# An attention kernel whose sets of chunks no longer cross batches: ten sets for nine, two more chunks transposed by the matrix engine, the last moved set issued by two engines

## The chip, the cores and the metric

The kernel runs on one core of one Trainium2 chip. The metric is the device time in microseconds of one execution; the number compared is the median of several runs.

## The reference

```python
B, C, N = 4, 128, 1024          # x is (4, 128, 32, 32), seen as (B, C, N)
h = group_norm(x, 8 groups) * gn_w + gn_b
q, k, v = qw @ h + qb, kw @ h + kb, vw @ h + vb      # per batch, [C, N]
attn = softmax(q^T k / sqrt(C), axis=-1)              # [N, N] per batch
out = x + pw @ (v attn^T) + pb
```

All arithmetic is in float32. The kernel folds qw and kw into one matrix and pw into the values, so that what is left per batch is a projection g, the values v, the scores g·h, the exponentials, and the product of values and exponentials, divided by the row sums.

## The kernel before

**Chunks and steps.** The 1,024 query rows of each of the 4 batches are cut into 8 chunks of 128: 32 chunks, handled in 32 steps. Step c computes the scores of chunk c on PE (six matmuls of 512 columns into one of two PSUM buffers S), and DVE drains them (L656: adds a row term, takes the minimum, writes s_sb). ACT then takes the exponential in place (L502) and sums the row.

**Turning the exponentials.** The product with the values needs the exponentials with keys on the partitions, so each chunk must be transposed. There are two ways.
- A direct chunk is transposed by PE in 8 pieces (`transpose_probs`, L404) into two PSUM banks, which ACT (L525) and DVE (L711) copy to pair_T.
- A moved chunk is transposed by DVE within 32x32 blocks (`transpose_blocks`, L665) into blocks, and DMAs then carry the blocks to other partitions, into pT (`move_set`, L189): 16 DMAs for a set, from 4 groups a of source partitions to 4 groups j of target partitions, each of the four a with its own semaphore.

**Sets.** Consecutive chunks form sets: `SETS = (2, 4, 4, 4, 4, 4, 4, 4, 2)`. The first and the last set are direct, the seven between are moved. The sets of four begin at chunks 2, 6, 10, ..., 26, so the sets from 6, 14 and 22 cross from one batch into the next. blocks and pT each have two buffers, used by sets in turn.

**Value units.** The product of a set is computed in units of 4 matmuls with 256 columns (8 instructions each in the profile, L377 for moved sets and L350 for direct ones), one unit per chunk, 32 in all. Unit m of a moved set runs in step m + LAG, with LAG = 8, after the scores of that step; units 0 and 1 run in steps 4 and 5. In a set inside one batch the first two units read only a = 0 and 1, so they wait for the first 8 DMAs alone, and the other two read a = 2 and 3. In a set that crosses, each unit takes two chunks of one batch and all four a, so that its first unit waits for all 16 DMAs.

**After the units.** The reciprocals of the row sums (rden, one per query row) are turned by PE into rows (`turn_rden`), copied by ACT (`copy_rows`), stored to DRAM by a DMA that ACT issues (L511), and spread back over all partitions by a DMA that SP issues (`spread_rows`, L197, into rden_bc). For the last two sets PE broadcasts them instead (L340). DVE multiplies (`divide`), POOL adds the residual (`add_residual`), and SP stores the set (`store_set`, L209).

**Queues.** Each engine's instructions are in an order written out by hand, and each engine runs its own in order; semaphores join them. SP's order is, for each set, move, spread, and then the store of the set two before. DVE does in step c, in this order: any divide, the drain of c, the copy of a direct chunk, the block transpose of c - 1, then small work and at some steps the statistics of the next batch. PE does the scores of c, then value tiles or a projection where they are due, then transposes, then a unit. In steps 0, 1, 2, 6 and 7 of a batch PE has such extra work, in 3, 4 and 5 nearly none.

Of the kernel before, what the change touches and what calls it, by code (L numbers as in the profile page):

```python
# [19 lines left out]
SETS = (2, 4, 4, 4, 4, 4, 4, 4, 2)  # L20

FIRST_UNIT_STEPS = (4, 5)
LAG = 8


def build(nc, x, vectors, weights, out):
# [22 lines left out]
    with ExitStack() as ctx:  # L49
# [14 lines left out]
        def is_direct(c):  # L64
            return c < SETS[0] or c >= DIRECT

        def direct_number(c):
            return c if c < SETS[0] else c - DIRECT + SETS[0]

        def columns(n):  # L70

            return slice(P * FIRST[n], P * (FIRST[n] + SETS[n]))

        def last_batch(n):
            return (FIRST[n] + SETS[n] - 1) // CH

        def crosses(n):

            return FIRST[n] // CH != last_batch(n)

        def divided_in(c):

            for n in range(LS - 2):
                last = FIRST[n] + SETS[n] - 1
                if c == (FIRST_UNIT_STEPS[last] + 3 if n == 0 else last + LAG + 1):
                    return n
            return None
# [43 lines left out]
        pair_T = sb("pair_T", [P, KT, 2, P])  # L131
# [7 lines left out]
        sums = [ACC[:, n % 2, 0:P * SETS[n]] for n in range(LS)] + [S[:, 1, 0:PN]]  # L139
        last_sums = [ACC[:, (LS - 1) % 2, 0:UW], ACC[:, LS % 2, 0:UW]]  # L140
# [25 lines left out]
        normed_ready, last_normed, out_ready, tail_out_ready, stored = map(sem, ("normed_ready", "last_normed", "out_ready", "tail_out_ready", "stored"))  # L166
        tp_psum = sem("tp_psum")
        pair_ready = [sem(f"pair_ready{f}") for f in range(HALVES)]

        xb_flat = xb[:, :, :].rearrange("p b n -> p (b n)")  # L170
# [7 lines left out]

        block = ctx.enter_context(nc.Block())

        @block.sync
        def _(sp):
            def move_set(n):
                sp.wait_ge(blocks_ready, FIRST[n + 1] - SETS[0])
                if n > 2:
                    sp.wait_ge(part_done, FIRST[n - 1])
                for a in range(NQ):
                    for j in range(NQ):
                        sp.dma_start(moved_view(n)[Q * j:Q * (j + 1), a].rearrange("p t n -> p (t n)"),  # L189
                                     blocks_view(n)[Q * a:Q * (a + 1), j].rearrange("p t c q -> p (t c q)"))\  # L190
                          .then_inc(moved[n % 2][a], 16)
# [8 lines left out]
            def store_set(n):  # L200
                if n < SPREAD_BY_DMA:
                    sp.wait_ge(out_ready, n + 1)
                else:
                    sp.wait_ge(tail_out_ready, 2 if n == LS else 3)
                at = P * FIRST[n]
                while at < P * (FIRST[n] + SETS[n]):
                    b, first = at // N, at % N
                    width = min(N, first + P * (FIRST[n] + SETS[n]) - at) - first
                    sp.dma_start(out[b, :, first:first + width], xb[:, b, first:first + width]).then_inc(stored, 16)  # L209
                    at += width  # L210
# [20 lines left out]
            sp.wait_ge(stored, 16 * (NS + sum(crosses(n) for n in range(NS))))  # L231

        @block.tensor
        def _(pe):
            def group_deviations(b):
                pe.wait_ge(chan_ready, b + 1)
                if b > 0:
                    pe.wait_ge(gvar_ready, b)
                if b > 1:
                    pe.wait_ge(rows_ready, 2 * (b - 1))  # L240
                pe.matmul(A0[:, 0:1], deviation[:, :], chan[:, 0:1], start=True, stop=True).then_inc(dmean_psum, 1)
# [26 lines left out]
            def project_g(b, f):  # L268
# [5 lines left out]
                else:  # L274
                    pe.wait_ge(v_ready, VP * b if f == 0 else VP * b + 2)
                    pe.wait_ge(row_ready, VP * b if f == 0 else VP * b + 2)
                pe.wait_ge(h_hi_ready, HALVES * b + f + 1)
# [51 lines left out]
            def turn_rden(n):  # L329
                pe.wait_ge(rden_ready, n + 1)  # L330
                pe.wait_ge(gvar_ready, min(FIRST[n + 1] // CH + 2, B))
                if n > 0:
                    pe.wait_ge(rows_ready, n)
                pe.transpose(A0[0:SETS[n], 0:P], rden[:, n % 2, 0:SETS[n]], ident[:, :]).then_inc(rows_psum, 1)
# [9 lines left out]
            def direct_unit(n, half):  # L344
                if half == 0:
                    for f in range(HALVES):
                        pe.wait_ge(pair_ready[f], 2 if n == 0 else 4)
                    pe.wait_ge(v_ready, VP if n == 0 else VP * B)
                for t in range(PT * half, PT * (half + 1)):
                    last = pe.matmul(sums[n], v[:, FIRST[n] // CH % 3, t, :], pair_T[:, t].rearrange("p d q -> p (d q)"),  # L350
# [3 lines left out]
            def moved_unit(n, u):  # L354
                b, part, half = (FIRST[n] + u) // CH, u // 2, u % 2
                if half == 0:
                    pe.wait_ge(v_ready, VP * (b + 1))
                    if u == 0 and n > 1:
                        pe.wait_ge(normed_ready, n - 1)
                    if u == 2 and n == LS - 1:  # L360
                        pe.wait_ge(normed_ready, n)
                    for a in range(NQ) if crosses(n) else (2 * part, 2 * part + 1):
                        pe.wait_ge(moved[n % 2][a], MOVED * ((n + 1) // 2))
                probs = moved_view(n)
                if crosses(n):

                    cs = slice(2 * Q * part, 2 * Q * (part + 1))
                    to = sums[n].rearrange("p (a n) -> p a n", a=NQ)[:, :, cs]
                    probs = probs[:, :, :, cs]
                elif n == LS - 1:  # L370
                    to = last_sums[part].rearrange("p (a n) -> p a n", a=2)
                    probs = probs[:, 2 * part:2 * (part + 1)]
                else:
                    to = sums[n][:, UW * part:UW * (part + 1)].rearrange("p (a n) -> p a n", a=2)
                    probs = probs[:, 2 * part:2 * (part + 1)]
                for t in range(PT * half, PT * (half + 1)):
                    last = pe.matmul(to, v[:, b % 3, t, :], probs[:, :, t, :], start=(t == 0), stop=(t == KT - 1))  # L377
                last.then_inc(part_done, 1)

            def value_unit(m):  # L380
                n, u = set_of(m)
                if n in (0, LS):
# [4 lines left out]
            def transpose_probs(c):  # L387
                k = direct_number(c)
                pe.wait_ge(probs_ready, c + 1)
                for f in range(HALVES):  # L390
                    to = (ACC[:, f, :] if c < SETS[0] else (A1, A0)[f])
# [28 lines left out]
            for c in range(STEPS):  # L420
# [12 lines left out]
                if c - 1 in FIRST[1:LS]:  # L433
                    turn_rden(FIRST.index(c - 1) - 1)
# [4 lines left out]
                if c - 2 in range(SETS[0]):  # L439
# [5 lines left out]
                if c >= LAG + SETS[0]:  # L445
# [12 lines left out]
            value_unit(FIRST[LS - 1] + 3)  # L458

        @block.scalar  # L460
        def _(act):
# [43 lines left out]
            def copy_rows(n):  # L505
# [3 lines left out]
                act.copy(rden_rows[0:SETS[n], n % 2, :], A0[0:SETS[n], 0:P]).then_inc(rows_ready, 1)  # L509
# [3 lines left out]

            def copy_rden(n):
                act.wait_ge(bc_psum, n - SPREAD_BY_DMA + 1)
                act.wait_ge(out_ready, n - 1)
                act.copy(rden_bc[:, n % 2, 0:P * SETS[n]], S[:, 0, BANK * (n % 2):BANK * (n % 2) + P * SETS[n]]).then_inc(bc_ready, 1)

            def copy_pair(c):
# [4 lines left out]
                frm = ACC[:, 0, :] if c < SETS[0] else A1[:, :]  # L524
                act.copy(pair_T[:, 0:PT, c % 2, :], frm.rearrange("p (t q) -> p t q", t=PT)).then_inc(pair_ready[0], 1)  # L525
# [18 lines left out]
            for c in range(STEPS):  # L544
# [11 lines left out]
                if i == 4 and c - 2 in FIRST[1:LS]:  # L556
                    copy_rows(FIRST.index(c - 2) - 1)
# [4 lines left out]
                if i == 7 and c - 1 in FIRST[1:LS]:  # L562
                    copy_rows(FIRST.index(c - 1) - 1)
                if c - 2 in range(SETS[0]):
# [3 lines left out]
                exponentials(c)  # L568
            copy_pair(STEPS - 1)
# [4 lines left out]
        def _(dve):  # L574
# [71 lines left out]
            def drain_scores(c):  # L646
# [4 lines left out]
                if c > 2:  # L651
                    if is_direct(c - 3):
                        dve.wait_ge(tp_psum, HALVES * (direct_number(c - 3) + 1))
                    else:
                        dve.wait_ge(blocks_ready, c - 2 - SETS[0])
# [3 lines left out]
            def transpose_blocks(c):  # L659
                n, k = set_of(c)  # L660
                dve.wait_ge(probs_ready, c + 1)
                if n > 2 and k == 0:
                    for a in range(NQ):
                        dve.wait_ge(moved[n % 2][a], MOVED * ((n - 1) // 2))
# [9 lines left out]
            def divide(n):  # L674
                dve.wait_ge(part_done, FIRST[n] + SETS[n] if n < LS else STEPS - 2)
# [5 lines left out]
                if n in (0, LS):  # L681
# [6 lines left out]
            def add_residual(n):  # L688
                dve.wait_ge(normed_ready, LS)
                xs = xb_flat[:, columns(n)]  # L690
                dve.tensor_tensor(xs, rden_bc[:, n % 2, 0:P * SETS[n]], xs, ALU.add).then_inc(tail_out_ready, 1)

            def finish_last_moved(part):
                n = LS - 1
                dve.wait_ge(part_done, FIRST[n] + 2 if part == 0 else STEPS)
                dve.wait_ge(bc_ready, 1)
                by_rden = rden_bc[:, n % 2, 0:P * GC].rearrange("p (c a q) -> p a c q", c=GC, a=NQ)[:, 2 * part:2 * (part + 1)]
# [169 lines left out]
```

## Time and profile before

| | us |
|---|---|
| median of 3 runs | 144.14 |
| lowest and highest | 143.91 and 144.76 |
| time of the profiled execution | 144.62 |
| its span, first to last instruction | 142.6 |
| PE busy | 130.1 (91%) |
| DVE busy | 99.5 (70%) |

The trace is of one execution. Times of rows are microseconds from the start of the span. PE's granted clock is 1.00 in every stretch.

### The profile page before, as it was taken

The page shows a single profiled execution, that of the slowest core. Times are in us where ns is not written, and L with a number is a line of the kernel's source. Part 1 is how long each engine was busy: PE and PEld are TensorE (multiplying, and loading weights), DVE is VectorE, ACT ScalarE, POOL GpSimd, SP SyncE. Part 2 cuts the span into 40 slices and gives each one's busy share as a digit, 9 for nine tenths or more (in the row PEclk, how much of TensorE's full clock was granted, in tenths as well). Part 3 has the DMA queues.
Part 4 walks back from the last instruction along what each step waited for, and adds up shares of the span by engine and source line. Part 5 has one row for each costly group of instructions (what it writes and reads, how often), then busy time and mean ns, then how long its engine had stood idle before and what let it go on. Part 6 is the DMA issues. An engine that isn't in the chain of part 4 may idle for free.

```text
span 142.6 us, 2014 instructions
## 1 busy us (share of the span) xinstructions
PE 130.1 (91%) x647; PEld 109.4 (77%) x647; DVE 99.5 (70%) x172; ACT 64.9 (46%) x112; POOL 26.1 (18%) x33
## 2 busy tenths in 40 slices
PE   5999999997779999799999995999999969999990
PEld 5997878865558887688888883888888847988880
DVE  0577779989998679679697789366977893521222
ACT  4053789564566653544436845054543333512000
POOL 5043050930202061100050323000030030003000
PEclk9999999999999999999999999999999999999999
DMA  4950000005996799499824997899509987979211
GB/s 147 306 210 0 0 5 0 27 12 115 214 205 168 171 211 203 118 205 210 195 93 92 202 209 200 202 204 210 162 0 205 209 195 202 205 161 223 78 37 74
DMA packets 9565, 20.98 MB, mean 147 GB/s; under 512 B 2362, under 2 KB 4052, under 8 KB 9556
## 3 DMA queue, kind: packets, MB, share of 16 engines
q1 hardware_dynamic: 8816, 20.59, 59.3%
q10 hardware_dynamic: 740, 0.28, 0.7%
q8 instruction: 5, 0.08, 0.2%
q14 instruction: 4, 0.03, 0.1%
HBM read 4.07 MB, written 2.11 MB: 43 GB/s over the span
## 4 chain that ended last, share of the span: by engine, by line
PE 56%; SPq 19%; DVE 11%; issue 6%; DMA 5%; POOL 0%; DVEq 0%; POOLq 0%
PE ACC L377 20%; SPq L189 19%; PE S L322 6%; DMA pT<-blocks 5%; PE S L326 5%; PE S L323 5%; PE S L266 5%; DVE blocks L665 4%; DVE s_sb L656 4%; PE A L302 3%; PE ACC L350 2%; PE S L350 2%; PE A L404 1%; PE ACC L404 1%; DVE bn L581 1%
## 5 line engine op out<-in xcount | busy, mean ns | idle before, releaser
L377 PE MATMUL ACC<-pT,v 128*128 128x256 f32 x224 | 52.8, 381 | 4.1 <-DMA pT<-blocks 4.1
L656 DVE TENSOR_SCALAR_CACHE_REDUCE s_sb<-S,row_term 128x1024 f32<-128x1024 f32 x32 | 41.0, 1281 | 20.7 <-PE S L326 20.2
L377 PEld LDWEIGHTS ACC<-pT,v 128*128 128x128 f32 x224 | 41.2, 190 | 10.9 <-issue 5.6
L502 ACT ACTIVATE s_sb<-s_sb,rowmin 128x1024 f32<-128x1024 f32 x32 | 36.8, 1151 | 20.9 <-DVE s_sb L656 19.9
L665 DVE STREAM_TRANSPOSE blocks<-s_sb 128x1024 f32<-128x1024 f32 x28 | 34.7, 1240 | 0.0
L322 PE MATMUL S<-h_hi,g_hi 128*128 128x512 f32 x64 | 30.2, 472 | 0.3 <-issue 0.3
L323 PE MATMUL S<-h_lo,g_hi 128*128 128x512 f32 x64 | 25.2, 393 | 0.0
L326 PE MATMUL S<-h_hi,g_lo 128*128 128x512 f32 x64 | 19.9, 392 | 0.0
L810 POOL TENSOR_TENSOR xb<-rden_bc,xb 128x512 f32<-128x512 f32 (+1 forms) x7 | 8.4, 1194 | 53.0 <-DVE rden_bc L685 45.5
L326 PEld LDWEIGHTS S<-h_hi,g_lo 128*128 128x128 f32 x64 | 12.0, 188 | 2.8
L322 PEld LDWEIGHTS S<-h_hi,g_hi 128*128 128x128 f32 x64 | 12.1, 189 | 2.5 <-issue 0.4
L494 ACT COPY v<-A 128x384 f32<-128x384 f32 (+1 forms) x12 | 5.3, 443 | 18.8 <-PE A L302 18.8
L323 PEld LDWEIGHTS S<-h_lo,g_hi 128*128 128x128 f32 x64 | 12.1, 189 | 2.0
L302 PEld LDWEIGHTS A<-wpv,h 128*128 128x128 f32 x64 | 8.4, 191 | 3.7 <-issue 2.6
L302 PE MATMUL A<-wpv,h 128*128 128x129 f32 x64 | 9.5, 281 | 1.3 <-DVE g_lo L630 1.1
L797 POOL TENSOR_TENSOR h_lo<-h,h_hi 128x1024 fp32r<-128x1024 f32 x3 | 7.2, 2398 | 17.8 <-ACT h L472 17.8
L266 PE MATMUL S<-ident 128*128 128x128 f32 x38 | 7.9, 363 | 1.6 <-POOL ident L814 1.6
L482 ACT ACTIVATE g_hi<-A,wpv 128x512 fp32r<-128x512 f32 x7 | 4.8, 689 | 9.4 <-PE A L284 9.4
L266 PEld LDWEIGHTS S<-ident 128*128 128x128 f32 x38 | 6.9, 265 | 1.6 <-POOL ident L814 1.6
L788 POOL TENSOR_TENSOR rstd<-gvar,minus_half 128x1 f32<-128x1 f32 x4 | 2.2, 552 | 30.6 <-DVE gvar L603 30.6
L581 DVE BATCH_NORM_STATS2 bn<-x_sb 128x6 f32<-128x512 f32 x8 | 5.3, 683 | 2.9 <-DMA x_sb<-x 2.9
L467 ACT ACTIVATE h_hi<-x_sb,gshift,gscale 128x1024 fp32r<-128x1024 f32 (+1 forms) x5 | 5.2, 1067 | 2.1 <-DVE gshift L614 1.6
(90 smaller groups left out, 103.4 us busy)
## 6 DMA issues: line engine op xcount, KB each, us to landing
pT<-blocks SPq DMA_DIRECT2D x112, 128.0 KB, 2.4
rden_bc<-row_store SPq DMA_DIRECT2D x6, 256.0 KB, 3.6
x_sb<-x SPq DMA_DIRECT2D x1, 1024.0 KB, 6.0
out<-xb SPq DMA_DIRECT2D x8, 128.0 KB, 2.8
out<-xb SPq DMA_DIRECT2D x4, 256.0 KB, 3.2
x_sb<-x SPq DMA_DIRECT2D x2, 256.0 KB, 3.0
x_sb<-x SPq DMA_DIRECT2D x1, 512.0 KB, 3.9
w_in<-weights ACTq DMA_DIRECT2D x2, 128.0 KB, 3.5
```

The lines of the kernel that those rows point to most:

```text
L189: sp.dma_start(moved_view(n)[Q * j:Q * (j + 1), a].rearrange("p t n -> p (t n)"), blocks_view(n)[Q * a:Q * (a + 1), j].rearrange("p t c q ...
L266: pe.matmul(S[:, 0, BANK:BANK + P], ident[:, :], ident[:, :], start=True, stop=True)
L302: last = pe.matmul(A1[:, PW1 * u:PW1 * (u + 1)], h[:, P * t:P * (t + 1)], wpv[:, 0:PW1], start=True, stop=True)
L322: pe.matmul(S[:, c % 2, ks], g_hi[:, qs], h_hi[:, b % 2, ks], start=True, stop=False)
L323: pe.matmul(S[:, c % 2, ks], g_hi[:, qs], h_lo[:, b % 2, ks], start=False, stop=False)
L326: last = pe.matmul(S[:, c % 2, ks], g_lo[:, qs], h_hi[:, b % 2, ks], start=False, stop=True)
L377: last = pe.matmul(to, v[:, b % 3, t, :], probs[:, :, t, :], start=(t == 0), stop=(t == KT - 1))
L502: act.activation(s_sb[:, c % 3, :], s_sb[:, c % 3, :], ACT.Exp, bias=rowmin[:, c % CH:c % CH + 1], scale=-1.0, accum_out=den[:, n % 2, k:k ...
L656: dve.tensor_scalar(s_sb[:, c % 3, :], S[:, c % 2, :], row_term[:, b % 2, i:i + 1], None, ALU.add, ALU.min, accum_out=rowmin[:, i:i + 1]). ...
L665: dve.transpose(blocks_view(n)[:, :, :, k, :].rearrange("p j t q -> p t j q"), s_sb[:, c % 3, :].rearrange("p (t j q) -> p t j q", t=KT, j ...
L797: pool.tensor_tensor(h_lo[:, b % 2, :], h[:, :], h_hi[:, b % 2, :].bitcast(F32), ALU.subtract).then_inc(h_lo_ready, 1)
L810: pool.tensor_tensor(xs, rden_bc[:, n % 2, 0:P * SETS[n]], xs, ALU.add).then_inc(out_ready, 1)
```

## The change

- **Sets.** Ten sets, `(2, 2, 4, 4, 4, 4, 4, 4, 2, 2)`, starting at chunks 0, 2, 4, 8, ..., 24, 28, 30. No set crosses a batch. Sets 0 and 1 (chunks 0 to 3) and set 9 (chunks 30 and 31) are direct; sets 2 to 7 of four chunks and set 8 (chunks 28 and 29) are moved. pair_T gets a second buffer, and the product of set 0 goes to A0, since ACC is in use by the transposes.
- **Lag.** LAG is 7. Units 0 to 3 run in steps 4 to 7, and unit m of a moved set in step m + 7, from unit 4 in step 11.
- **Last moved set.** Set 8 is moved in 16 DMAs of half the size: SP issues the 8 for target groups j = 0 and 1, ACT the 8 for j = 2 and 3 (`move_last_set`), after the exponentials of step 30. Its two units read all four a each and run last; the direct set runs ahead of them.
- **Rows of rden.** One more turn, copy, row store and spread. They sit at fixed steps: the even sets in steps 3 and 4 of a batch, the odd ones in steps 5 and 6. The order on SP becomes move, store, spread. So the spread of sets 2, 4 and 6 comes just ahead of the next set's move. Sets 0 and 1 are divided in steps 7 and 9, later ones in the step of their first chunk plus 11. The last set is finished in one piece.

```diff
-SETS = (2, 4, 4, 4, 4, 4, 4, 4, 2)
-FIRST_UNIT_STEPS = (4, 5)
-LAG = 8
+SETS = (2, 2, 4, 4, 4, 4, 4, 4, 2, 2)
+PAIRS = 4
+FIRST_UNIT_STEPS = (4, 5, 6, 7)
+FIRST_DIVIDED_STEPS = (7, 9)
+LAG = 7
...
             def move_set(n):
-                sp.wait_ge(blocks_ready, FIRST[n + 1] - SETS[0])
-                if n > 2:
+                sp.wait_ge(blocks_ready, FIRST[n + 1] - PAIRS)
+                if n > 3:
                     sp.wait_ge(part_done, FIRST[n - 1])
                 for a in range(NQ):
-                    for j in range(NQ):
...
+                    for j in range(NQ if n < LS - 1 else NQ // 2):
+                        move_piece(sp, n, a, j)
...
             spread_rows(0)
-            move_set(1)
             spread_rows(1)
+            move_set(2)
             store_set(0)
-            for n in range(2, LS):
+            store_set(1)
+            spread_rows(2)
+            for n in range(3, LS):
                 move_set(n)
+                if n > 3:
+                    store_set(n - 2)
                 if n < SPREAD_BY_DMA:
                     spread_rows(n)
-                if n > 2:
-                    store_set(n - 2)
...
             def moved_unit(n, u):
-                b, part, half = (FIRST[n] + u) // CH, u // 2, u % 2
+                b, size = FIRST[n] // CH, SETS[n]
+                a0, width, half = (2 * (u // 2), 2, u % 2) if size == GC else (0, NQ, u)
...
                 if half == 0:
+                    for a in range(a0, a0 + width):
+                        pe.wait_ge(moved[n % 2][a], MOVED * (n // 2))
...
-                if c - 1 in FIRST[1:LS]:
-                    turn_rden(FIRST.index(c - 1) - 1)
+                if i == 3 and (b == 0 or c > CH):
+                    turn_rden(2 * b if b > 0 else 0)
+                if i == 5:
+                    turn_rden(2 * b + 1)
...
-                if c - 2 in range(SETS[0]):
+                if c - 2 in range(PAIRS):
                     transpose_probs(c - 2)
...
             value_unit(STEPS - LAG)
+            value_unit(STEPS - LAG + 1)
             transpose_probs(STEPS - 1)
-            for m in range(STEPS - LAG + 1, FIRST[LS - 1]):
+            for m in range(STEPS - LAG + 2, FIRST[LS - 1]):
                 value_unit(m)
             broadcast_rden(LS - 1)
             broadcast_rden(LS)
+            value_unit(DIRECT)
+            value_unit(DIRECT + 1)
             value_unit(FIRST[LS - 1])
             value_unit(FIRST[LS - 1] + 1)
-            value_unit(DIRECT)
-            value_unit(DIRECT + 1)
-            value_unit(FIRST[LS - 1] + 2)
-            value_unit(FIRST[LS - 1] + 3)
...
+            def move_last_set():
+                n = LS - 1
+                act.wait_ge(blocks_ready, DIRECT - PAIRS)
+                act.wait_ge(part_done, FIRST[n - 1])
+                for a in range(NQ):
+                    for j in range(NQ // 2, NQ):
+                        move_piece(act, n, a, j)
...
                 exponentials(c)
+                if c == DIRECT:
+                    move_last_set()
```

## Rows read from the trace of the kernel before

**Rows 1.** The page, part 5: costliest groups (busy, mean ns | idle before, releaser).

```profile
L377 PE MATMUL ACC<-pT,v 128*128 128x256 f32 x224 | 52.8, 381 | 4.1 <-DMA pT<-blocks 4.1
...
L502 ACT ACTIVATE s_sb<-s_sb,rowmin 128x1024 f32<-128x1024 f32 x32 | 36.8, 1151 | 20.9 <-DVE s_sb L656 19.9
```

**Rows 2.** Timeline of DVE (start, us): drains of steps 7, 8, 10, 12, 14, 15, 28, 30, 31.

```profile
22.55 0.69 DVE L711 COPY pair_T<-ACC 128x512 f32<-128x512 f32 x1
...
23.15 1.24 DVE L665 STREAM_TRANSPOSE blocks<-s_sb 128x1024 f32<-128x1024 f32 x1
...
33.00 1.27 DVE L656 TENSOR_SCALAR_CACHE_REDUCE s_sb<-S,row_term 128x1024 f32<-128x1024 f32 x1
...
37.19 1.28 DVE L656 TENSOR_SCALAR_CACHE_REDUCE s_sb<-S,row_term 128x1024 f32<-128x1024 f32 x1
...
42.91 1.27 DVE L656 TENSOR_SCALAR_CACHE_REDUCE s_sb<-S,row_term 128x1024 f32<-128x1024 f32 x1
...
50.14 1.28 DVE L656 TENSOR_SCALAR_CACHE_REDUCE s_sb<-S,row_term 128x1024 f32<-128x1024 f32 x1 [0.77 <-PE S L326]
...
56.35 1.28 DVE L656 TENSOR_SCALAR_CACHE_REDUCE s_sb<-S,row_term 128x1024 f32<-128x1024 f32 x1
...
61.34 1.28 DVE L656 TENSOR_SCALAR_CACHE_REDUCE s_sb<-S,row_term 128x1024 f32<-128x1024 f32 x1 [1.84 <-PE S L326]
...
110.14 1.28 DVE L656 TENSOR_SCALAR_CACHE_REDUCE s_sb<-S,row_term 128x1024 f32<-128x1024 f32 x1 [0.77 <-PE S L326]
...
116.34 1.28 DVE L656 TENSOR_SCALAR_CACHE_REDUCE s_sb<-S,row_term 128x1024 f32<-128x1024 f32 x1
...
121.34 1.28 DVE L656 TENSOR_SCALAR_CACHE_REDUCE s_sb<-S,row_term 128x1024 f32<-128x1024 f32 x1 [2.49 <-PE S L326]
```

**Rows 3.** Chain that ended last, in order of time: the last crossing set, the end.

```profile
105.86 0.51 SPq L189
106.41 0.59 SPq L189
...
115.28 2.52 DMA pT<-blocks
117.94 1.97 PE ACC L377 x8
...
139.29 0.44 DVE rden_bc L698
```

**Rows 4.** Timeline of SP's DMA queue: moves (L189), spreads (L197), stores (L209).

```profile
43.21 0.45 SPq L209 DMA_DIRECT2D out<-xb  x1
...
56.04 0.51 SPq L197 DMA_DIRECT2D rden_bc<-row_store  x1
58.83 10.03 SPq L189 DMA_DIRECT2D pT<-blocks  x16
...
99.48 1.57 SPq L209 DMA_DIRECT2D out<-xb  x1
...
118.82 10.96 SPq L189 DMA_DIRECT2D pT<-blocks  x16
```

**Rows 5.** Chain that ended last, in order of time: a direct chunk, scores, a unit.

```profile
21.41 0.87 PE ACC L404 x8
22.28 0.23 PE S L322
...
23.67 1.73 PE ACC L350 x8
```

**Rows 6.** Windows: busy time of each engine, PE's clock, share of the DMA engines, GB/s.

```profile
89.00:99.00 10.00, 10.00 (x53) 8.62 (x52) 5.55 (x9) 3.58 (x7) 0.00 (x0) 1.00 0.91 204
...
2.00:6.00 4.00, 4.00 (x20) 3.91 (x20) 1.60 (x3) 1.22 (x2) 0.88 (x3) 1.00 0.93 287
```

**Rows 7.** DMA issues by line: KB each, median us from issue to landing.

```profile
out<-xb SPq DMA_DIRECT2D x8, 128.0 KB, 2.8
out<-xb SPq DMA_DIRECT2D x4, 256.0 KB, 3.2
```

More of the change, by code:

```diff
@@ L64, in is_direct @@
         def is_direct(c):
-            return c < SETS[0] or c >= DIRECT
+            return c < PAIRS or c >= DIRECT
         def direct_number(c):
-            return c if c < SETS[0] else c - DIRECT + SETS[0]
+            return c if c < PAIRS else c - DIRECT + PAIRS
         def columns(n):
[L72 to L79, printed above, removed]
+            b, i = FIRST[n] // CH, FIRST[n] % CH
+            return b, slice(P * i, P * (i + SETS[n]))
         def divided_in(c):
-            for n in range(LS - 2):
-                last = FIRST[n] + SETS[n] - 1
-                if c == (FIRST_UNIT_STEPS[last] + 3 if n == 0 else last + LAG + 1):
+            for n in range(SPREAD_BY_DMA):
+                if c == (FIRST_DIVIDED_STEPS[n] if n < 2 else FIRST[n] + SETS[n] + LAG):
                     return n
@@ L203, in store_set @@
                 else:
[L204 to L210, printed above, removed]
+                    sp.wait_ge(tail_out_ready, 1 if n == LS else 2)
+                b, cs = columns(n)
+                sp.dma_start(out[b, :, cs], xb[:, b, cs]).then_inc(stored, 16)
             for f in range(HALVES):
@@ L230, in _ @@
             store_set(LS - 1)
-            sp.wait_ge(stored, 16 * (NS + sum(crosses(n) for n in range(NS))))
+            sp.wait_ge(stored, 16 * NS)
         @block.tensor
@@ L354, in moved_unit @@
             def moved_unit(n, u):
-                b, part, half = (FIRST[n] + u) // CH, u // 2, u % 2
-                if half == 0:
[L357 to L375, printed above, removed]
+                b, size = FIRST[n] // CH, SETS[n]
+                a0, width, half = (2 * (u // 2), 2, u % 2) if size == GC else (0, NQ, u)
+                if u == 0:
+                    pe.wait_ge(v_ready, VP * (b + 1))
+                    if n > 2:
+                        pe.wait_ge(normed_ready, n - 1)
+                    else:
+                        for f in range(HALVES):
+                            pe.wait_ge(pair_ready[f], PAIRS)
+                if half == 0:
+                    for a in range(a0, a0 + width):
+                        pe.wait_ge(moved[n % 2][a], MOVED * (n // 2))
+                to = sums[n].rearrange("p (a n) -> p a n", a=NQ)[:, a0:a0 + width]
                 for t in range(PT * half, PT * (half + 1)):
-                    last = pe.matmul(to, v[:, b % 3, t, :], probs[:, :, t, :], start=(t == 0), stop=(t == KT - 1))
+                    last = pe.matmul(to, v[:, b % 3, t, :], moved_view(n)[:, a0:a0 + width, t, :], start=(t == 0), stop=(t == KT - 1))
                 last.then_inc(part_done, 1)
@@ L561, in _ @@
                     copy_v(b + 1, 0)
-                if i == 7 and c - 1 in FIRST[1:LS]:
-                    copy_rows(FIRST.index(c - 1) - 1)
-                if c - 2 in range(SETS[0]):
+                if c - 2 in range(PAIRS):
                     copy_pair(c - 2)
@@ L747, in _ @@
                 drain_scores(c)
-                if c - 2 in range(SETS[0]):
+                if c - 2 in range(PAIRS):
                     copy_pair(c - 2)
```

104 lines of the change are left out of this document (54 added, 50 removed).

## The prediction

> **What bounds the kernel now.** I read the costliest groups first, then the waits, then the times at which DVE starts to drain each step's scores, since a drain starts as soon as PE has finished them. I write T8 for the start of the drain of step 8. PE is busy 91% of the span, so what it does and where it stands still sets the time. Its only long wait on another unit's data is for moved blocks, 4.1 us in 3 waits [rows 1]. The drains show where: the steps from T12 to T14 take 3.1 us each ((56.35 - 50.14) / 2), while T14 to T15 takes 4.99 and T30 to T31 takes 5.00 [rows 2]. The chain of the last such place reads: SP issues 16 DMAs from 105.86, 0.59 us and a gap of 0.04 each, the sixteenth lands 2.52 us after 115.28, and PE starts at 117.94 [rows 3]. So a crossing set waits 12.1 us from the first issue (117.94 - 105.86). The eight DMAs that a set inside a batch needs first would be there 8 x 0.635 = 5.1 us sooner, 7.0 us after the first issue. The places are the three crossing sets, in steps 14, 22 and 30.
>
> A step of PE with scores and a unit costs 3.10 to 3.12; with a projection 3.82 (a projection of three matmuls like the scores' adds 0.7). Step 14 therefore stood still for 4.99 - 3.82 = 1.2, step 30 for 5.00 - 3.11 = 1.9, and step 22 lies between, about 1.7. Together 4.8 us.
>
> The first moved stage is different. In steps 7 to 10 DVE is the bound: PE has no units, and T7 to T8 takes 4.19 [rows 2] for a drain, a block transpose and the statistics of a batch.
>
> **The change part by part.** I follow the new order step by step, with durations of these rows, in three stretches.
>
> *Start to T12.* Two more chunks are transposed by PE, each 0.87 [rows 5], so 1.74 more; DVE exchanges two block transposes of 1.24 for two copies of 0.69 [rows 2] (1.1 less); ACT gets two copies of 0.6. Until 23.67, the start of unit 0 now, nothing changes. From there PE is the bound. Step 4 is transposes 0.87, unit 1.73, next scores 1.39 (23.67 - 22.28) [rows 5]: 3.99 to 27.7. Step 5 again 3.99 to 31.7. Step 6 is projection 0.7, unit, scores: 3.82 to 35.5. That is T7, against 33.00 [rows 2]. The copies of DVE and ACT lie under this PE time. The new wait of the projection, for ACT's second copy of rows, is met: ACT has it about 1 us ahead. From T7 DVE is the bound again: T8 = 35.5 + 4.2 = 39.7. T8 to T10 takes 5.7 now (42.91 - 37.19); the reciprocal of set 2 and the divide of set 1 come into it, about 0.4 as an estimate from the 0.3 to 0.4 of their kind, so T10 = 45.8. PE then has value tiles (0.5) and scores (1.4) and is done with those of step 11 at about 47.9. The set 2 move starts when the blocks of chunk 7 are done, 2.5 after T8, at 42.2, and its first half is there at 42.2 + 7.0 = 49.2. So lag 7 gives a wait of 1.3 in step 11. Then unit 1.97 (the form after a wait) [rows 3] and scores 1.39: T12 = 52.5, against 50.14, but with one unit (1.73) more done.
>
> *T12 to T28.* It is 60.0 now [rows 2]; two stops (1.2 + 1.7) go, 57.1. The new deadlines: a set that starts at step 4 of a batch gets its first unit 3 steps after its move begins, with all extra work of steps 0 to 2 between: 11.2 from the drain, ready at 2.5 + 7.0 = 9.5, slack 1.7. A set that starts a batch has the steps 4 to 6 and value tiles between: 10.6 against 9.5, slack 1.1. Just ahead of that move stands now a 256 KB spread. The nearest row of such a neighbour is the store behind a spread, 1.57 to issue in place of the 0.45 of other stores [rows 4], 1.1 lost; this eats the slack and no more. I put 0.3 for both sets, between 0 and 2.2 (twice the lateness). T28 = 52.5 + 57.1 + 0.3 = 109.9, against 110.14. The second halves are needed 5 steps after, over 15.5 against 14.6, and pass.
>
> *T28 to the last matmul.* Now 139.26 - 110.14 = 29.1. New: the move of set 7 starts at T28 + 2.5. PE reaches the chunk 30 transposes at T28 + 9.1 (three steps of 3.1), unit 24 at 10.0 with the first half there at 9.5, and unit 26 at 13.4. The second half is there at 2.5 + 12.1 = 14.6: a new stop of 1.1. In mid-kernel two steps with extra work lie between the halves and cover this; here they do not, since the units come back to back. From 14.6: unit 1.97, transposes 0.87, unit 1.73, broadcasts 0.44 (four PE transposes, half of the eight that take 0.87 [rows 5]), four units 6.92. That is 26.5. I add 0.3, since the issue of a move takes from 10.03 to 10.96 [rows 4] and this one has a spread ahead.
>
> And then ACT. It starts its 8 DMAs at the end of the exponentials of step 30 (drain 1.3, exponentials 1.15 and their sum 0.15 [rows 1]), T30 + 2.6 = T28 + 8.8, when SP has issued 10 of the 16 of set 7. No row shows two queues at once, so I bound it. From below 0: if SP's 0.635 us per DMA is issue time, ACT's go beside them; for this speaks that each issue takes the same 0.59 [rows 3]. From above 512 KB at 204 GB/s, 2.5 us: if the DMA engines are the limit; for this speaks their share of 0.91 [rows 6]. Between them, loads from DRAM ran at 287 GB/s with a share of 0.93 [rows 6]: then SP's last 768 KB and ACT's 512 KB take 4.5 in place of 3.8, 0.7 later. I take 1.2 for the middle, leaning on the last. The tail is 26.5 + 0.3 + 1.2 = 28.0.
>
> The Trainium skill, DMA: Bandwidth & Descriptors, section Issuing engines are not separate DMA queues, says that DMAs of different issuing engines run on the same 16 engines and interleave, and that issuing from several saves only the sequencer's time. The share of 0.91 agrees, the equal issue times leave it open; by that rule the term is 2.5 in place of 1.2.
>
> SP's half of set 8 comes after set 7, a store and a spread: first issue near T28 + 15, last landing 15 + 8 x 0.63 + 2 = 22, or 23.5 with the sharing. PE wants it at 28.0 - 3.5 = 24.5. It is covered by units 26, 27, 30 and 31, with 1 to 2.5 to spare.
>
> *End.* Now 142.6 - 139.26 = 3.3. The last multiply and add are unchanged in size, the last store is 128 KB in place of 256 KB, 0.4 sooner by median [rows 7]; I take 0.2: 3.1.
>
> **Sum.** 52.5 + 57.4 + 28.0 + 3.1 = 141.0 against the span of 142.6: 1.6 less. Of the 4.8 us of stops, 1.3 + 1.3 come back in step 11 and at unit 26, 1.2 to ACT's traffic, and 1.5 net to PE's two extra transposes less the two spared broadcasts; the small terms make up the rest. The profiled execution took 144.62, 0.48 above the median; I take the difference to the median: 144.14 - 1.6 = 142.5.
>
> **The rivals.**
> - *The two queues run beside each other.* The sharing term is 0 to 0.4. Equal issue times speak for it, the share of 0.91 against it. Time 144.14 - 1.6 - 1.0 = 141.5.
> - *Full sharing.* The DMA engines are the limit and set 7 is 2.5 late. Time 142.5 + 1.3 = 143.8. It is the case of the Trainium skill's section cited above.
> - *Spreads ahead of moves.* The first halves of sets 3 and 5 come 2.2 late, not 1.1, since the spread stands wholly ahead of them on the queue. PE stops 1.1 at each. Time 142.5 + 1.9 = 144.4. Against it: the move at 58.83, 2.8 us after a spread, issued in its usual 10.03 [rows 4]. For it: the new spread is not 2.8 but 0.5 us ahead.
> - *Slower: ACT is held by its issues.* Copy and exponentials of chunk 31 stand behind ACT's 8 DMAs, and PE needs them at T28 + 18.0. At 0.63 each ACT is free at 13.9 and the exponentials are done 1.9 later at 15.8, covered by unit 26. At the 1.57 of an issue in a full queue [rows 4] they are done at 8.8 + 12.6 + 1.9 = 23.3, 5.3 late: 147.8. It decides the sign from an issue of about 1.1 us on. For it: the queue is fullest just there. Against: the moves of 16 issue in 10.03 to 10.96, so at most one of 16 can be that long.
>
> **How the numbers follow.** Forecast (sharing 0.7 to 1.7, 141.9 to 143.1) 0.36, side by side 0.22, full sharing 0.18, spreads 0.12, ACT held 0.12. Half a per cent, 0.7 us, is about what a measurement of this kernel can tell from no change. Faster than 143.4 are the first two cases and part of the third: 0.63. Same: the rest of full sharing and most of the spreads, 0.22. Slower, above 144.9: ACT held, and stops that add up, 0.15. The range of 8 in 10 goes from 140.7 (side by side, and no small terms) to 145.2 (the spreads with full sharing), with most of ACT held left out.
>
> **What would show it.** Right: units in steps 15, 19, 23 and 27 start with no wait; T7 near 35.5, T12 near 52.5, T28 near 110; a wait for DMA of about 1.3 in step 11; one of 1 to 3.5 ahead of unit 26; last matmul near 138. If the DMAs of set 7 issued after ACT has begun land later than 2.5 us or are issued more slowly than 0.63, the engines are shared. Wrong: PE waiting for exponentials of chunk 31, waits in steps 15 and 23, or a T12 above 53.5, which would mean that DVE bounds the start more than I have it.

## The result: slower, with runs far apart

| | median | lowest and highest | runs |
|---|---|---|---|
| before | 144.21 us | 143.91 and 144.76 | 4 |
| after | 148.75 us | 147.36 and 150.77 | 4 |

The ratio is 1.022, 95% interval 1.0165 to 1.0275. It leaves out runs more than 1.5% above the fastest of the same kernel, here 149.96 and 150.77; since the two that are left have a mean PE clock of 0.977 too, against 0.995 or more in the kernel before, the clock is no matter of the slow runs alone, and I speak of all runs. With four more runs taken beside the experiments the changed kernel's times are 144.9, 145.1, 147.4, 147.5, 149.1, 149.9, 150.0 and 150.8, with a median of 148.3: the two lowest are only 0.7 and 0.9 above the median of the kernel before. The kernel before has stayed within 143.9 and 145.4 in all its runs. The forecast was 142.5, with a range from 140.7 to 145.2.

The profiled execution after took 150.77, its span is 148.8. On its page the granted clock of PE in the 40 slices (PEclk) is not at its highest throughout, as it was before:

```profile
PE   5999999999987399999999999999999999189991
PEclk9999999999999969999999999999999999956999
...
L376 PE MATMUL ACC<-pT,v 128*128 128x256 f32 x208 | 52.6, 400 | 6.4 <-DMA pT<-blocks 6.4
```

L376 is the line of the moved units, L377 before. There are 16 fewer instructions, but the mean rose from 381 to 400 ns, and the wait for blocks from 4.1 us in three places to 6.4 in two [rows 1]. Two slices of low PE busy, a 3 and a 1, are each followed by slices of low clock.

The drains of steps 7, 8, 10, 12, 28 and 31, against [rows 2]:

```profile
35.91 1.28 DVE L666 TENSOR_SCALAR_CACHE_REDUCE s_sb<-S,row_term 128x1024 f32<-128x1024 f32 x1 [0.40 <-PE S L324]
...
39.83 1.28 DVE L666 TENSOR_SCALAR_CACHE_REDUCE s_sb<-S,row_term 128x1024 f32<-128x1024 f32 x1
...
45.94 1.27 DVE L666 TENSOR_SCALAR_CACHE_REDUCE s_sb<-S,row_term 128x1024 f32<-128x1024 f32 x1
...
55.83 1.28 DVE L666 TENSOR_SCALAR_CACHE_REDUCE s_sb<-S,row_term 128x1024 f32<-128x1024 f32 x1 [4.87 <-PE S L324]
...
112.89 1.28 DVE L666 TENSOR_SCALAR_CACHE_REDUCE s_sb<-S,row_term 128x1024 f32<-128x1024 f32 x1 [0.77 <-PE S L324]
...
122.33 1.28 DVE L666 TENSOR_SCALAR_CACHE_REDUCE s_sb<-S,row_term 128x1024 f32<-128x1024 f32 x1
```

T7, T8 and T10 are within about 0.4 us of the forecast 35.5, 39.7 and 45.8. T12 to T28 takes 57.06; the forecast was 57.4. Nearly all that was lost lies in two places: T10 to T12 and the tail after T28. The windows around them (busy time of PE, PE weight loads, DVE, ACT, POOL, then the clock, the share of the DMA engines, GB/s):

```profile
48.00:50.00 2.00, 0.26 (x2) 0.00 (x0) 2.00 (x6) 1.81 (x4) 0.00 (x0) 1.00 0.95 205
50.00:52.00 2.00, 1.21 (x4) 1.09 (x5) 0.97 (x1) 2.00 (x3) 0.00 (x0) 0.84 0.91 199
52.00:54.00 2.00, 2.00 (x6) 1.54 (x5) 0.00 (x0) 0.36 (x2) 1.71 (x1) 0.50 0.92 202
54.00:56.00 2.00, 2.00 (x8) 1.61 (x8) 0.17 (x1) 0.00 (x0) 0.64 (x1) 0.81 0.94 230
120.00:126.00 6.00, 5.98 (x32) 5.06 (x31) 4.19 (x8) 1.24 (x2) 1.27 (x1) 1.00 0.99 237
126.00:130.00 4.00, 0.87 (x5) 0.42 (x3) 0.17 (x1) 1.72 (x3) 0.00 (x0) 0.98 1.01 214
130.00:132.00 2.00, 1.30 (x3) 1.15 (x4) 0.00 (x0) 0.00 (x0) 0.00 (x0) 0.50 0.85 239
132.00:134.00 2.00, 2.00 (x6) 1.55 (x6) 0.00 (x0) 0.00 (x0) 0.00 (x0) 0.50 0.55 140
```

PE stands still, and when or shortly after its blocks come it works at a clock of 0.50, the lower of its two levels (1.2 in place of 2.4 GHz). PE's own timeline, and for the rest the chain, give the price:

```profile
50.79 3.20 PE L376 MATMUL ACC<-pT,v 128*128 128x256 f32 x8 [2.53 <-DMA pT<-blocks]
...
130.70 3.75 PE L376 MATMUL ACC<-pT,v 128*128 128x256 f32 x8 [3.83 <-DMA pT<-blocks]
```

```profile
134.46 1.71 PE A L403 x8
136.16 2.06 PE ACC L376 x8
```

A unit after a wait took 1.97 before [rows 3]; here unit 4 took 3.20 and unit 26 took 3.75. On the chain the scores after unit 4 took 1.80 (from 53.99 to 55.79) against 1.39, the transposes of chunk 31 took 1.71 against 0.87, and unit 27 took 2.06 against 1.73. That is 1.23 + 0.41 = 1.6 us at step 11 and 1.78 + 0.84 + 0.33 = 3.0 us in the tail: 4.6 us for the clock alone.

The moves of set 7, SP's queue and ACT's:

```profile
115.37 11.26 SPq L173 DMA_DIRECT2D pT<-blocks  x16
...
128.73 5.17 SPq L173 DMA_DIRECT2D pT<-blocks  x8
```

```profile
121.69 5.61 ACTq L173 DMA_DIRECT2D pT<-blocks  x8
```

and, on the chain, the fourth issue of that move and its end:

```profile
117.19 1.51 SPq L173
...
125.20 0.59 SPq L173
125.83 4.74 DMA pT<-blocks
130.70 3.75 PE ACC L376 x8
```

ACT begins at T28 + 8.80, as forecast. SP's sixteenth DMA lands 4.74 us after the start of its issue, not 2.5. It is also issued about 1 us later than in most other moves, but that is not ACT's doing: 0.9 of it comes from the fourth issue, which took 1.51 and ended 3 us before ACT began its own. Unit 26 starts 15.3 us after the move's first issue, where 13.6 was forecast (12.1 + 0.3 + 1.2).

### The profile page after: what moved, and what is told of

The parts are those of the page before. It is cut to its first block, busy times and chain, and to the rows that moved or that the text cites. A ratio compares the mean times of both kernels' runs of the same rounds, so it can differ in the third digit from the quotient of the medians.

```text
span 148.8 us, 2061 instructions
## 1 busy us (share of the span) xinstructions
PE 135.7 (91%) x662; PEld 114.9 (77%) x662; DVE 98.2 (66%) x172; ACT 65.8 (44%) x115; POOL 26.8 (18%) x34
## 4 chain that ended last, share of the span: by engine, by line
PE 75%; SPq 10%; DMA 5%; DVE 4%; issue 4%; POOL 0%; DVEq 0%; POOLq 0%
PE ACC L376 27%; SPq L173 10%; PE S L320 8%; PE S L321 8%; PE S L324 8%; PE S L262 5%; DMA pT<-blocks 5%; PE A L300 4%; PE ACC L403 2%; PE A L357 2%; PE S L357 2%; DVE blocks L675 2%; PE ACC L357 1%; PE A L403 1%; DVE s_sb L666 1%
## 5 line engine op out<-in xcount | busy, mean ns | idle before, releaser
L376 PE MATMUL ACC<-pT,v 128*128 128x256 f32 x208 | 52.6, 400 | 6.4 <-DMA pT<-blocks 6.4
L376 PEld LDWEIGHTS ACC<-pT,v 128*128 128x128 f32 x208 | 40.4, 201 | 13.6 <-issue 7.5
L675 DVE STREAM_TRANSPOSE blocks<-s_sb 128x1024 f32<-128x1024 f32 x26 | 32.2, 1240 | 0.0
L320 PE MATMUL S<-h_hi,g_hi 128*128 128x512 f32 x64 | 30.9, 482 | 0.3 <-issue 0.3
L809 POOL TENSOR_TENSOR xb<-rden_bc,xb 128x512 f32<-128x512 f32 (+1 forms) x8 | 9.1, 1134 | 74.5 <-DVE rden_bc L695 62.3
L321 PEld LDWEIGHTS S<-h_lo,g_hi 128*128 128x128 f32 x64 | 12.3, 192 | 2.1
L796 POOL TENSOR_TENSOR h_lo<-h,h_hi 128x1024 fp32r<-128x1024 f32 x3 | 7.1, 2379 | 12.9 <-ACT h L472 12.9
L695 DVE TENSOR_TENSOR rden_bc<-ACC,rden_bc 128x512 f32<-128x512 f32 (+1 forms) x7 | 4.5, 642 | 3.9 <-PE ACC L376 3.9
L533 ACT COPY pair_T<-A 128x512 f32<-128x512 f32 x2 | 1.2, 586 | 11.8 <-PE A L403 6.2
```

The source lines that it names most:

```text
L320: pe.matmul(S[:, c % 2, ks], g_hi[:, qs], h_hi[:, b % 2, ks], start=True, stop=False)
L321: pe.matmul(S[:, c % 2, ks], g_hi[:, qs], h_lo[:, b % 2, ks], start=False, stop=False)
L376: last = pe.matmul(to, v[:, b % 3, t, :], moved_view(n)[:, a0:a0 + width, t, :], start=(t == 0), stop=(t == KT - 1))
L675: dve.transpose(blocks_view(n)[:, :, :, k, :].rearrange("p j t q -> p t j q"), s_sb[:, c % 3, :].rearrange("p (t j q) -> p t j q", t=KT, j ...
L809: pool.tensor_tensor(xb[:, b, cs], rden_bc[:, n % 2, 0:P * SETS[n]], xb[:, b, cs], ALU.add).then_inc(out_ready, 1)
```

## The experiments

All are the changed kernel with one edit, unless another is named, and leave nothing of the computation out. Where matmuls of no use are added, their results are not read. "Clock" is PE's mean granted clock of a run. Ratios are against the runs of the kernel before that were taken beside each group of experiments: medians 144.82 (experiments 1 to 4), 144.30 (5 to 8) and 144.56 (9 to 11).

**1. PE kept at work in both waits.**

```diff
+                if c == LAG + PAIRS:
+                    pe.wait_ge(v_ready, 2 * VP)
+                    pe.wait_ge(row_ready, 2 * VP)
+                    keep_warm_in_wait(9, A1[:, 0:P])
                 if c >= LAG + PAIRS:
...
+            pe.wait_ge(rowmin_ready, STEPS - 1)
+            keep_warm_in_wait(15, S[:, 0, BANK:BANK + P])
             value_unit(STEPS - LAG + 1)
```

> The changed kernel with small matmuls of no use (128x128, about 0.22 us each) put where PE stands still: 9 ahead of unit 4 in step 11 and 15 ahead of unit 26. The waits for the moved blocks stay as they are; only PE is kept at work in them. Theory clock: the two stops let the granted clock fall from 1.00 to 0.50, and unit 4 (3.20 in place of 1.97), the scores after it (1.80 in place of 1.39), unit 26 (3.75), the transposes of chunk 31 (1.71 in place of 0.87) and unit 27 (2.06 in place of 1.73) cost 4.6 us by that. Then this kernel has a clock of 1.00 throughout and takes 143 to 144.5. Theory late blocks: the whole loss is that the blocks land late, and the clock is no matter. Then it takes what the changed kernel takes, 147 to 148.

Ten runs: 144.6 to 145.6 in eight, 146.9 and 147.0 in two, median 144.94, ratio 1.0019 (0.9991 to 1.0046). The mean clock is 0.996 to 1.000 in every run, where the changed kernel has 0.965 to 0.988. In the profile PE's clock is 1.00 throughout, and the chain of the tail is:

```profile
124.83 3.35 PE S L266 x30
128.18 1.73 PE ACC L380 x8
129.91 0.87 PE A L407 x8
130.78 1.73 PE ACC L380 x8
```

The 15 useless matmuls (two instructions each in the profile) take 3.35 us, and behind them unit 26, the transposes and unit 27 are back at 1.73, 0.87 and 1.73. The waits themselves are still there: the last DMA of set 7 lands 14.8 us after the first issue (112.94 to 127.76; 15.2 in the first trace), 0.4 before the useless matmuls end, and the kernel is no faster than the one before. Eight runs lie 0.1 to 1.1 us above what I had expected. What the two runs near 147 lost, at a clock of 0.996 and 1.000, I do not know.

**2. Set 8 issued by SP alone.**

```diff
-                    for j in range(NQ if n < LS - 1 else NQ // 2):
+                    for j in range(NQ):
...
-                if c == DIRECT:
-                    move_last_set()
```

> The changed kernel with all 16 half-size DMAs of set 8 issued by SP, none by ACT. Theory sharing: ACT's eight DMAs made the move of set 7 late (issue 1.0 us longer than 10.0, last landing 4.7 in place of 2.5 us), so here the last DMA of set 7 lands about 12.1 to 12.6 us after the first issue, PE stops about 1.2 ahead of unit 26 in place of 3.8, and the clock stays up there. But set 8 is issued wholly after set 7: 16 issues at 0.63 would end near T28 + 25 and PE would stop ahead of unit 28 by up to 4 us, unless half-size DMAs are issued faster. Theory no sharing: the second half of set 7 lands as late as before.

Four runs, 145.9 to 149.2, median 147.5, ratio 1.0161 (1.0062 to 1.0261). SP's queue and PE's timeline:

```profile
113.05 10.60 SPq L173 DMA_DIRECT2D pT<-blocks  x16
...
124.87 10.01 SPq L173 DMA_DIRECT2D pT<-blocks  x16
```

```profile
125.94 1.97 PE L376 MATMUL ACC<-pT,v 128*128 128x256 f32 x8 [1.64 <-DMA pT<-blocks]
...
136.48 5.38 PE L376 MATMUL ACC<-pT,v 128*128 128x256 f32 x16 [2.08 <-DMA pT<-blocks]
```

Without ACT's DMAs unit 26 starts 12.9 us after the first issue (125.94 - 113.05), 2.4 sooner than in the trace of the changed kernel, and keeps the full clock after its stop of 1.64 (1.2 was expected). Step 11 has a stop of 1.72 with no fall after it. The loss has moved, as expected: the 16 half-size DMAs are issued no faster than full ones, 10.01 us for 16, set 8 comes 2.1 us late, and its two units take 5.38 in place of 3.47, at a clock that has fallen again.

**3. ACT's DMAs one step later.**

```diff
-                if c == DIRECT:
+                if c == STEPS - 1:
                     move_last_set()
```

> The changed kernel with ACT's eight DMAs of set 8 issued after the exponentials of step 31 in place of step 30. Theory sharing: ACT starts about 3 us later (near T28 + 12), when SP has issued all but one or two of set 7, so that set lands nearly undisturbed, PE stops 1.2 to 2 us ahead of unit 26 in place of 3.8, the clock stays at 1.00 there, and the time is 3 to 5 us below the changed kernel: 143 to 144.5. Theory no sharing: the stop ahead of unit 26 stays near 3.8, and the time near 147.5.

Ten runs, 142.8 to 147.9, median 145.47, in groups by their clock: four runs with 1.000 took 142.8, 143.5, 143.8 and 144.1, five with 0.988 or 0.976 took 145.4 to 146.4, one with 0.977 took 147.9. The expected 143 to 144.5 holds for three of them, and a fourth is below. The four with the full clock alone, against the kernel before, give a ratio of 0.9925 (0.9888 to 0.9962). In the profile (146.38, both drops) unit 26 starts 13.25 us after the first issue (127.60 - 114.35), close to SP alone. So the overlap with ACT's DMAs is most of what made set 7 late, and the runs that kept their clock lie at 143.5 in the mean, 1.0 above the forecast. The stops stay near the edge: 2.1 us in step 11 and 2.0 at unit 26, each followed by a fall in this execution.

**4. Units 2 and 3 in steps 9 and 11.**

```diff
-FIRST_UNIT_STEPS = (4, 5, 6, 7)
-FIRST_DIVIDED_STEPS = (7, 9)
+FIRST_UNIT_STEPS = (4, 5, 9, 11)
+FIRST_DIVIDED_STEPS = (7, 12)
```

> The changed kernel with units 2 and 3 moved from steps 6 and 7 to steps 9 and 11 (and the divide of set 1 from step 9 to 12), where PE has nothing to do; unit 3 then stands ahead of unit 4 in the wait for set 2. Theory clock: PE has work in the wait, the stop in step 11 falls from 2.5 to 1 or less and the clock does not fall there; T12 comes at 52 to 53 in place of 55.8, and the time is about 2.5 to 3 us less than the changed kernel's in runs that have the drop in step 11 (144.5 to 145.5). Rival: in the fast runs of the changed kernel the clock does not fall at step 11 anyway, and the time stays above 146.5.

The expected gain of 2.5 to 3 us did not come: four runs, 147.6 to 149.7, ratio 1.0263. T12 is at 53.50 with no drop at step 11, as expected, but SP's store of set 1 now waited for the divide in step 12 and for POOL, and held the move of set 3 to 56.5: unit 8 waited 1.14 us in step 15, where no wait had been. The tail's drop stayed. This run was of use for the two combined versions below.

**5. The changed kernel again.**

> The changed kernel once more, unaltered (a blank line more), to be beside the others on one chip. Theory clock: its runs fall into groups by the mean clock; those near 0.977 have one of the two drops shorter or missing, those near 0.966 have both. 147.3 to 150.8, as at first.

144.94, 145.08, 149.08 and 149.88, so faster at best than I had expected; the ratio of 1.0043 (0.9992 to 1.0094) rests on the first two. The profile is of the 145.08, the case to hold beside the first trace:

```profile
49.14 1.97 PE L377 MATMUL ACC<-pT,v 128*128 128x256 f32 x8 [1.06 <-DMA pT<-blocks]
...
126.58 3.35 PE L377 MATMUL ACC<-pT,v 128*128 128x256 f32 x8 [3.10 <-DMA pT<-blocks]
```

Here the stop in step 11 is 1.06 us, not 2.53, the clock stays, and T12 is at 52.50, the forecast to the digit. In the first trace one of the first eight issues had taken 2.07 us in place of 0.59. The tail's stop and drop are there: last matmul 30.3 us after T28, against 28.0 forecast and 32.7 in the first trace.

**6. Useless matmuls in the first wait alone** (the first of the two edits of experiment 1).

> The changed kernel with matmuls of no use in the first wait alone: 9 ahead of unit 4 in step 11, none at unit 26. Theory clock: the drop in step 11 costs 1.2 for unit 4 and 0.4 for the scores after it, 1.6 in all, and where the stop is long the wait for the blocks stays. So 1.6 less than the changed kernel in runs that had that drop: about 145.8 to 147.5, and T12 at 53.5 to 54 in place of 55.8. Theory late blocks: no change.

Four runs, 147.1 to 149.3, with clocks of 0.977 and 0.988. Step 11 behaves: unit 4 takes 1.73, T12 is at 53.96 in place of 55.83. But the tail of this profile is the worst of all: unit 26 waits 4.33 us and starts 16.4 us after the first issue: SP's sixteen issues take 12.42, 1.5 of which come from one issue of 2.08 before ACT began, and ACT's DMAs run beside the later ones. The totals missed what was expected (145.8 to 147.5) in three runs of four, so the gain at step 11 shows in the trace and not in the times.

**7. The wait of the tail covered by work.** PE transposes chunk 31 before unit 25 and runs the direct units before 26 and 27; ACT issues after the copies of chunk 31; rden_bc has a third buffer, so that set 9 can be divided ahead of set 7 (DVE, POOL and SP follow that order).

```diff
-            value_unit(STEPS - LAG)
-            value_unit(STEPS - LAG + 1)
             transpose_probs(STEPS - 1)
-            for m in range(STEPS - LAG + 2, FIRST[LS - 1]):
-                value_unit(m)
+            value_unit(STEPS - LAG)
             broadcast_rden(LS - 1)
             broadcast_rden(LS)
             value_unit(DIRECT)
             value_unit(DIRECT + 1)
+            for m in range(STEPS - LAG + 1, FIRST[LS - 1]):
+                value_unit(m)
...
-                if c == DIRECT:
-                    move_last_set()
             copy_pair(STEPS - 1)
+            move_last_set()
```

> The changed kernel with another order at its end: ACT issues its eight DMAs after the copies of chunk 31, PE transposes chunk 31 ahead of unit 25, and the direct units 30 and 31 run ahead of units 26 and 27, so that some 4.4 us of work lie in the wait for the second half of set 7 (a third buffer of rden_bc for the last set makes this possible). Nothing is left out. If the wait at unit 26 (3.8 us) and its clock drop (3.0 us) are what the tail loses, both go, save that PE may wait up to 1 us for the exponentials of chunk 31: T28 to the last matmul 25.5 to 27 in place of 32.7, and 142 to 143.5 in all, or 140.5 to 141.5 in runs where step 11 keeps its clock. If the tail is held by something else, for one the DMAs of set 8, it stays above 29.

Four runs: 140.32 and 141.15 with a clock of 1.000, 143.39 and 143.87 with 0.988, about as expected. The first two give the ratio 0.9747 (0.9690 to 0.9804); the fall in the other two, which have no trace, is probably that of step 11, which this edit leaves open. The chain of the tail in the profile (140.32):

```profile
120.17 1.25 ACT s_sb L501 x2
121.42 0.04 issue
121.46 1.09 PE A L403 x8
122.55 1.73 PE ACC L376 x8
124.28 0.44 PE S L344 x4
124.72 3.46 PE S L357 x16
128.18 6.96 PE ACC L376 x32
```

From 121.46 PE does not stop: 32 instructions in 6.96 us are units 26, 27, 28 and 29 with no wait. T28 (109.40) to the last matmul is 25.7 us, against 29.1 before and 30.3 to 32.7 in the changed kernel.

**8. Both remedies.** The tail of experiment 7, the units of experiment 4, and the store of set 1 behind the move of set 3.

> The tail of the kernel just named, and with it units 2 and 3 in steps 9 and 11, with the store of set 1 behind the move of set 3 on SP, since in the run with late units the move of set 3 was held to 56.5 by that store and PE waited in step 15. No useless work, nothing left out. Both drops of the clock and most of both waits should be gone: T12 at 52.5 to 53.5, no wait in step 15, the clock at 1.00, and 140 to 141.5 in all, with runs close together. If the waits are not what costs, it takes what the changed kernel takes.

141.84, 141.62, 142.30 and 141.72, all with a clock of 1.000; ratio 0.9826 (0.9789 to 0.9863). Unit 4 waits 0.19:

```profile
48.45 1.89 PE L356 MATMUL ACC<-pair_T,v 128*128 128x256 f32 x8
50.53 1.97 PE L375 MATMUL ACC<-pT,v 128*128 128x256 f32 x8 [0.19 <-DMA pT<-blocks]
```

Unit 3 is in front of it. The last of the eight DMAs landed 3.79 us after its issue in this execution, so without unit 3 the stop would have been 2.1 us (an estimate, 1.89 + 0.19). It is slightly slower than expected (140 to 141.5), and than the two runs of experiment 7 with the full clock; T12 is at 53.92. What it gains is that no run of four lost the clock.

**9 and 10. The kernel before with a longer stop, bare and filled.** PE also waits for the reciprocals of set 7 ahead of unit 22.

```diff
+                if c == DIRECT:
+                    pe.wait_ge(rden_ready, LS)
                 if c >= LAG + SETS[0]:
```

> The kernel before with one more wait: PE waits ahead of unit 22 in step 30 for the reciprocals of set 7 too, which are written about 0.9 us after the moved blocks land, so that this stop is 2.5 to 2.7 us long in place of 1.6. Theory clock: a stop of that length after busy steps lets the clock fall as in the changed kernel: unit 22 takes 3 or more in place of 1.97, and the whole is 0.9 + 1.5 to 2.5 slower than the kernel before, 146.5 to 147.5. Rival: the clock falls only where PE was thin for longer, as in steps 8 to 11 of the changed kernel or in 3.8 us at its unit 26; then only the stop itself is added, 145.1.

> The same, with 11 matmuls of no use (2.5 us) in the stop. The stop's end is unchanged and the clock stays at 1.00: 145.1 by both theories. What the kernel with the bare stop takes above this one is the price of the clock alone.

The bare stop is 2.60 us long in the profile, where it was 1.64 before, and after it:

```profile
116.00:118.00 2.00, 0.05 (x1) 0.00 (x0) 1.94 (x4) 0.58 (x1) 1.26 (x1) 1.00 0.82 186
118.00:120.00 2.00, 1.35 (x3) 1.17 (x4) 0.60 (x2) 0.66 (x2) 0.00 (x0) 0.53 0.69 203
120.00:122.00 2.00, 2.00 (x7) 1.59 (x7) 0.00 (x0) 0.00 (x0) 0.00 (x0) 0.61 0.93 201
```

Its ten runs fall into three groups: 145.1 to 145.4 with a clock of 1.000 (four), 146.6 to 147.3 with 0.988 (four), 148.5 and 148.9 with 0.973 (two). The theory of the clock had put the runs at 146.5 to 147.5, its rival at 145.1; both occur. So one edit that adds less than 1 us of waiting makes the kernel before behave like the changed one, and the fall costs 1.5 us (146.8 against 145.3, the middles of the groups), in some executions and not in others. With the stop filled, all four runs have 0.996 to 1.000, at 145.6, 145.7, 147.2 and 148.8. The profile is of the last: its first drain comes at 17.40 us, 4.0 later than in the bare kernel's, so that this run lost its time before the first scores. The 147.2 I cannot explain, and 145.1 had been expected of all four. The clock column tells the two kernels apart; the times of the filled one alone would be too few.

**11. One unit moved in place of two.** As experiment 8, with units in steps 4, 5, 6 and 11.

> The changed kernel with the new tail, unit 2 left in step 6 and unit 3 alone moved, from step 7 to step 11 ahead of unit 4 (divide of set 1 in step 12, its store behind the move of set 3). Unit 2 in step 9 cost about 1 us in the run with both units moved, since it held the scores of step 10 and so DVE (T10 46.7 after T7 35.8, against 45.6 after 35.6). So T12 at 52.5 to 53.2 in every run, no clock drop, and 140.5 to 141.5, 0.5 to 1 less than with both units moved. Rival: the stop in step 11 opens again, with drops in some runs and a spread of 2 us or more.

Six runs, 140.95 to 142.85, median 142.03, ratio 0.9811 (0.9766 to 0.9855); clocks of 0.997 to 1.000. The expected 140.5 to 141.5 came in two of six, and it is not better than experiment 8 (0.9826): its profile, of the slowest run, has T12 at 54.11, not 52.5 to 53.2, since unit 4 waited 0.88 behind unit 3. The wait in step 11 is set by when the blocks land, not by where unit 3 stood before.

## Why the prediction was wrong

**The failed step: every stop of PE was priced at its own length.** The forecast says of step 11 "Then unit 1.97 (the form after a wait)" and scores 1.39, and of the tail "From 14.6: unit 1.97, transposes 0.87, unit 1.73". Both stand behind a stop, and there the clock was 0.50. The kernel before has three stops, priced at 1.2 to 1.9 us; in its trace PE idles for 0.93, 1.51 and 1.64 there, and each first unit takes 0.24 more than the others. No fall follows them, and I took 1.3 and 2.6 for the same sort. Experiments 1, 6, 9 and 10 show the clock as a cause by itself: filling the stop removes the fall, and lengthening one stop of the kernel before brings it on in six runs of ten. In the profiled execution it makes 4.6 of the 7.8 us between forecast and span (148.8 - 141.0); that is the slowest of the eight runs. By the medians of all runs, filling both waits takes the changed kernel from 148.3 to 144.9. The Trainium skill, TensorE: Matmul & The Clock Gate, section HAM oscillation — how this bites in real kernels, tells of a kernel whose PE was throttled anew by each wait for a DMA; the windows above agree for these two waits, but here not each wait was followed by a fall. I did not weigh that rule, though the forecast itself put a stop of 2.6 us into the tail.

**Sharing: right in kind, mis-sized, and a long issue left out.** The forecast for unit 26 was 12.1 + 0.3 + 1.2 = 13.6 us after the first issue of set 7, with 0.3 for a spread ahead of the move and 1.2 for sharing, from bounds of 0 and 2.5. It is 12.9 with SP alone (experiment 2), 13.25 with ACT 8.3 us behind SP (experiment 3), and 14.55, 15.3, 15.25 and 16.4 with ACT 6 us behind it (experiment 5, the first trace, experiments 4 and 6). Not all of that is sharing. In each of these six traces one of the third to fifth DMAs of the move, all before ACT begins, took 1.06 to 2.08 us to issue in place of 0.59. Without that excess it is 12.3 with SP alone and 13.9, 14.4, 14.0 and 14.9 with ACT, so the sharing comes to 1.6 to 2.6, near the upper bound, and the rival of full sharing, at 2.5, had this term about right. The long issue costs 0.5 to 1.5, where 0.3 was put for all of it. Whether the spread ahead of the move makes that issue long, no run tested. The equal issue times of 0.59 spoke for no sharing; most of them held while the last landing went from 2.5 to 4.7. The section of the Trainium skill, DMA: Bandwidth & Descriptors, that was cited says the engines are shared; the landings agree.

**The variation of DMAs: one number was forecast for a wait that varies.** The wait of step 11 was forecast as 1.3. It was 1.06, 1.06, 1.72, 2.06 and 2.53 in five traces (experiments 5, 7, 2 and 3, and the first), by one issue of up to 2.07 us or one landing of 3.5, and the clock fell after the last two alone. In the kernel before, such an issue stands in two moves (1.11 and 1.51 us) and no fall came after either.

**The account beside the sum.** The forecast says that of the 4.8 us of stops 1.3 + 1.3, 1.2 and 1.5 come back, and that small terms make up the rest. Those are 5.3, more than 4.8, so that a gain of 1.6 would need 2.1 us of other terms. The sum of 141.0 does not use this account; it goes by stretches of time.

**Right.** T7, T8, T10 and, where the clock stayed and no issue was long, T12 (52.50); no wait in steps 15, 19, 23 and 27 in the trace after, so the spreads ahead of moves cost nothing there; 57.06 for T12 to T28; ACT's start. The rival "ACT held by its issues" did not come true: its eight DMAs took 5.61 us to issue, and the exponentials of chunk 31 were done at 129.1, before unit 26 could start at 130.7. The runs of experiment 3 with a clock of 1.00 (142.8 to 144.1) are about the kernel that I had forecast.

**Where the gain went.** The three stops did go. In their place came two, of 2.5 and 3.8 us, and each drew a fall of the clock behind it. A kernel with the even sets can be faster than the one before: 25.7 us of tail in experiment 7, and about 1.8% less time in experiments 8 and 11. But these have the reordered tail as well, and the kernel before was not run with such a tail, so what the even sets give by themselves is shown only by the four runs of experiment 3 with the full clock, 0.75%.

## What to carry to other kernels

Price a stop of the matrix engine as its length plus what the work behind it may lose at the lower clock, and look at whether the stop varies from run to run: removing three short stops is no gain if two long ones come. Put work that needs nothing of the late transfer into the wait (here the direct units), rather than let the engine stand. A second queue that issues beside the first does not make the first one's transfers cheaper; start it when the urgent move has been issued.

## What the runs showed of the hardware that was not expected

- The clock's fall was not the same in each run of one kernel: with a stop of about 2.6 us put into the kernel before, the mean clock shows it in six runs of ten. In the traces, one execution of each kernel, bare stops of 1.7 us and less had no fall behind them, and those of 2.0 to 4.3 all had one.
- A DMA of 64 KB takes as long to issue as one of 128 KB with the same number of rows: 16 in 10.01 us, against 10.03 [rows 4].
- Single issues of 1.0 to 2.1 us turn up among issues of 0.59: 31 of them in the 82 moves of sixteen in all traces, never two in one move, and also where ACT moves no blocks. Their cause is not known.
